# Zero fill of the first pair table from ScalarE's queue in group 0, and pair adds from group 9

## The reference, cut to what matters

```python
msg = relu(x[src] + edge_attr @ We + be)            # layer 0, graph
agg = segment_sum(msg, dst, num_segments=2500)
...
out = segment_sum((x @ W)[src] * norm, dst)         # layer 1: needs the count of (src, dst) in list 1
...
agg = segment_sum(h[src] * alpha, dst)              # layer 2, feed-forward: count of (src, dst) in list 2
```

## Time and profile before

| | |
|---|---|
| time before, median of 3 runs | 6491.18 us (6484.43 to 6493.86) |
| profiled execution, its own time | 6495.75 us |
| span of its profile | 6493.9 us |
| busy: PE, DVE, POOL, ACT | 5235.9, 3690.0, 3034.0, 1601.6 us |
| first `add` of the edges stage, last one | 83.94 us, 1697.36 us |

### The profile page before, as it was taken

The page is one execution under the profiler, slowest core; times in us unless marked ns, Lnnn a source line. Parts: engine busy times, 40 slices in busy tenths (PEclk is TensorE's granted clock), DMA queues, the critical chain, the costliest instruction groups (busy, mean ns, idle before and its releaser), DMA issues.

```text
span 6493.9 us, 83030 instructions
## 1 busy us (share of the span) xinstructions
PE 5235.9 (81%) x25932; PEld 3282.1 (51%) x25932; DVE 3690.0 (57%) x7654; ACT 1601.6 (25%) x2625; POOL 3034.0 (47%) x2048
## 2 busy tenths in 40 slices
PE   4677777777699898989569798776657998998899
PEld 3555555555455575558557566761113333222366
DVE  6777777787511202120235400979986997777732
ACT  1111111111222201220132121245541003555421
POOL 2577777788888878877777885000000000000000
PEclk8887887788799988999788699989988999999889
DMA  7765565644555596559799766944340001222100
GB/s 172 171 119 109 110 120 114 94 65 64 57 20 15 8 124 41 15 23 125 90 159 112 56 48 61 206 105 120 105 115 28 28 24 46 72 73 70 53 17 25
DMA packets 537605, 515.96 MB, mean 79 GB/s; under 512 B 262861, under 2 KB 494230, under 8 KB 531390
## 3 DMA queue, kind: packets, MB, share of 16 engines
q1 hardware_dynamic: 275694, 422.98, 29.8%
q0 software_dynamic: 261696, 90.13, 22.6%
HBM read 359.18 MB, written 153.71 MB: 79 GB/s over the span
## 4 chain that ended last, share of the span: by engine, by line
PE 46%; DVE 13%; issue 6%; SPq 5%; DMA 3%; ACT 1%; DVEq 0%; POOL 0%; ACTq 0%; POOLq 0%; PEldq 0%
PE PS L909 6%; PE PS L881 6%; PE PS L2033 6%; SPq L187 5%; PE PS L1901 5%; DVE WORK L1785 4%; PE PS L1270 4%; DVE MXS L1942 4%; PE PS L892 4%; PE PS L1562 3%; PE PS L1061 2%; PE PS L1050 2%; PE PS L245 2%; PE PS L1922 1%; PE PS L1252 1%
## 5 line engine op out<-in xcount | busy, mean ns | idle before, releaser
L642 POOL DMA_INDIRECT pairs<-PAIR_CNT,PAIR_IDX x1364 | 2159.8, 1583 | 559.1 <-issue 438.9
L469 DVE SCALAR_TENSOR_TENSOR XT<-PS,ROWS,XT 128x512 f32<-128x512 f32 (+1 forms) x1364 | 937.6, 743 | 148.1 <-PE PS L461 137.7
L999 DVE SCALAR_TENSOR_TENSOR X<-PS,G,X 125x256 f32<-125x256 f32 x440 | 193.0, 479 | 827.0 <-PE PS L909 786.2
L682 POOL DMA_INDIRECT sums<-WORK,ROWS x340 | 529.7, 1558 | 251.4 <-issue 189.0
L2088 DVE SCALAR_TENSOR_TENSOR WORK<-WORK 125x1000 f32<-125x1000 f32 x400 | 462.1, 1197 | 203.9 <-ACT WORK L2063 199.5
L1901 PE MATMUL PS<-ROWS 32*125 32x500 f32 x3200 | 455.8, 639 | 28.8 <-DVE MXS L1942 19.2
L1942 DVE TENSOR_REDUCE MXS<-PS 125x4 f32<-125x2000 f32 x200 | 438.8, 2235 | 41.6 <-PE PS L1922 37.6
L2063 ACT ACTIVATE WORK<-PS 125x1000 f32<-125x1000 f32 x400 | 380.0, 1002 | 329.3 <-PE PS L2023 329.3
L510 PE MATMUL PS<-WORK,IDENT 125*125 125x256 f32 x680 | 257.6, 467 | 237.9 <-DMA WORK<-x_table,WORK 237.7
L461 PEld LDWEIGHTS PS<-IDENT,ROWS 128*128 128x128 f32 (+1 forms) x2728 | 434.1, 226 | 30.0 <-issue 0.7
L461 PE MATMUL PS<-IDENT,ROWS 128*128 128x128 f32 (+1 forms) x2728 | 433.4, 312 | 0.0
(11 more groups left out here) (284 smaller groups left out, 7438.5 us busy)
## 6 DMA issues: line engine op xcount, KB each, us to landing
WORK<-pairs SPq DMA_DIRECT2D x400, 218.8 KB
pairs<-ROWS SPq DMA_DIRECT2D x75, 976.6 KB
WORK<-pairs SPq DMA_DIRECT2D x48, 1093.8 KB
WORK<-pairs SPq DMA_DIRECT2D x80, 546.9 KB
pairs<-PAIR_CNT,PAIR_IDX POOLq DMA_INDIRECT x1364
WORK<-pairs SPq DMA_DIRECT2D x40, 382.8 KB
XT<-pairs SPq DMA_DIRECT2D x12, 1093.8 KB
mask_t<-ROWS SPq DMA_DIRECT2D x40, 273.4 KB
```

The lines of the kernel that those rows point to most:

```text
L469: st.go(dve.scalar_tensor_tensor(KEY_JUNK[0:n, q, 0:SUPER * n], PS[0:n, bank, 0:SUPER * n], cols[0:n, q:q + 1], weights, ALU.is_equal, ALU ...
L642: pool.indirect_dma_start(table, bass.IndirectOffsetOnAxis(idx[:, n:n + 1], 0), cnt[:, n:n + 1], None, compute_op=ALU.add).then_inc(sem(do ...
L682: pool.indirect_dma_start(sums[c], bass.IndirectOffsetOnAxis(SROW[:, k % 8:k % 8 + 1], 0), SUMMED[:, k % 8, :], None, compute_op=ALU.add). ...
```

## The change

The 25 zero transfers of `pairs1` leave SP's loop. ACT issues them in group 0, after the copy of the sum of each step: 6, 6, 6 and 7 of them, with constant addresses. SP still issues the zero transfers of `pairs2` in the same iterations as before, and still the small one at the end of each table. `PG` is 9, not 13: three columns of list 1 are added in each of the groups 9 to 12 too, so `IN1` = 228, and 112 columns are left for `pairs_pool`.

```diff
-        PG, IN_GROUP = 13, 3
+        PG, IN_GROUP = 9, 3
...
+        def zero(eng, table, name, at):
+            rows = table[0:PAIRS, :].rearrange("(r p f) o -> r p (f o)", r=ZP, p=ZL)
+            rows = rows[at] if isinstance(at, int) else rows[ds(at, 1)].rearrange("r p f -> p (r f)")
+            eng.dma_start(rows, ZERO[0:ZL, 0:PAIRS // (ZP * ZL)]).then_inc(sem(name), 16)
...
             with sp.Fori(0, ZI) as i:
                 group(i * 2 + 1, 1)
                 group(i * 2 + 2, 0)
-                for n in range(ZP // ZI):
-                    zero(pairs1, "zeroed1", i * (ZP // ZI) + n)
...
                 for c in range(2):
-                    zero(pairs2[c], "zeroed2", i - ZI)
+                    zero(sp, pairs2[c], "zeroed2", i - ZI)
...
                     act.activation(SUMMED[0:P, s, :], PS[0:P, 4 + b, 0:AGG], ACT.Copy).then_inc(sem("sum_kept"), 1)
+                    if isinstance(g, int):
+                        for at in range(ZP * j // GR, ZP * (j + 1) // GR):
+                            zero(act, pairs1, "zeroed1", at)
```

More of the change, by code:

```diff
@@ L430, in edges_sp @@
                              ZERO[0:64, 0:2 * SUPER]).then_inc(sem("zeroed1" if table is pairs1 else "zeroed2"), 16)
-            def zero(table, name, at):
-                sp.dma_start(table[0:PAIRS, :].rearrange("(r p f) o -> r p (f o)", r=ZP, p=ZL)[ds(at, 1)]
-                             .rearrange("r p f -> p (r f)"), ZERO[0:ZL, 0:PAIRS // (ZP * ZL)]).then_inc(sem(name), 16)
             with sp.Fori(0, ZI) as i:
```

## The result

The changed kernel takes 6507.35 us (median of 17 runs, 6490.49 to 6523.03), the kernel before 6487.48 us (17 runs, 6466.78 to 6503.61): ratio 1.0033, interval 1.0021 to 1.0044. It is slower by a third of a per cent, some 20 us. That is inside the stated range (6478 to 6510) but not in the likeliest case; it fell to the 0.20 of "slower".

A forecast was written before the change was run, and what follows sets the result against it. POOL, saturated in the edges stage, was taken as the bound. Floor + 22.4 us, stall 91.6 to 69 = - 22.6, everything else 0: about 0, rounded to + 1, 6492 us on the median's scale; range 6478 to 6510.

The forecast's parts named there:

- the likeliest case: Whole kernel: a time within 0.2% of before, given 0.67.
- the 0.20 of "slower": Whole kernel: chance that it gets slower, from 0.09 + 0.10 for two rivals and 0.01 of the forecast's own spread.
- Both signs of being wrong: Fill burst and first 13 groups: steps not near 8 us, or stall not within some 10 us of 69.
- Who ends the stage, and that nobody waits for POOL later: Edges stage ends with POOL's last `add`; 22.4 us less POOL work after it is worth nothing.
- Twelve pair adds on the path: Groups 9 to 12, ahead of the last `add`: 12 x 1.87 = + 22.4 us.
- ScalarE's issues: Group 0, ACT's queue: 0.4 us for two zero transfers and 2.2 for 23, together 51 us.
- Steps in the burst: During the zero fill: POOL gets 10.5 steps done, at 8.2 us a step where its floor is 3.18.
- The step that failed: Groups 0 to 8: POOL's floor is 12.7 us a group, 114.5 us in all.
- The transfers have more time to drain: Groups 9 to 12: with pair adds between `add`s, `pairs2` zeroing costs 1.1 us a group, 4 us instead of 10.1.
- the stall did not go with the bytes: Rival on the fill: 16.3 us per 5 MB in any burst, stall 85.5, + 16 us, 6507; chance 0.10.
- POOL got no more room in a long burst: Rival on the fill: 5.5 us a step, 17 steps in the burst, - 19 us, 6472; chance 0.10.
- ScalarE was not held for the whole fill: Rival on ACT's queue: issues at drain pace hold ACT throughout, + 10 us, or + 26 at 226 GB/s; chance 0.18.

The follow-up runs named there:

- spread kernel: Also cited as (6): kernel before, PG = 13, each of SP's five `pairs1` zero transfers per iteration waiting for its own step; 6430.32 us, ratio 0.9929.
- 2: Changed kernel with PG back at 13, so only the zero fill from ScalarE remains, against the kernel before; 6496.32 us, ratio 1.0035.
- 5: Kernel before with PG = 85, no pair add in the edges stage, the wait for `zeroed1` moved to `pairs_pool`; 6968.36 us, one run.

## Why the prediction was right or wrong

The time lies in the range, but the mechanism isn't the one that was forecast, and that is in part luck. The forecast was a stall that shrinks from 91.6 to 69 us and so pays for the twelve pair adds. Counted in the same way, the stall after is 363.33 - 83.94 - 187.7 = 91.7 us: it didn't shrink at all. Both signs of being wrong that the prediction named have come, this one and the steps in the burst: 8 of them in the 98 us from 83.94 to 181.88, 12.2 us each and not near 8. The range reached up to 6510 for two rivals, and neither is what happened.

- **Who ends the stage, and that nobody waits for POOL later**: right. The slowdown is about the 17.9 us of the stage's end, and that POOL's last pair add came 21 us earlier bought nothing.
- **Twelve pair adds on the path**: right in kind. The prediction let groups 9 to 12 go from 61.0 to 73.2 + 4 = 77 us; they take 80.1.
- **ScalarE's issues**: 51 us predicted, 53.1 measured. Of the 25 MB, 20.06 went out in 90 to 175 us and the last 0.7 by about 182, near the forecast 180. The 6.27 us an issue, taken from the earlier trace rows for the pace of draining, were a misreading: it is the longest of four issues that took 13.68 us together, 3.4 each. The sum didn't use it.
- **Steps in the burst**: 10.5 predicted, with the ninth `add` (step 8) at 181.88 only 8 are done. That is 2.5 x 3.18 = 8 us. It is the hold: VectorE's row numbers of group 1 are missing for 23.5 us, VectorE waits for TensorE, and TensorE for the messages behind the issues (41.8 us).
- **The step that failed**: "Groups 0 to 8 cost 9 x 12.7 = 114.5 us". POOL runs at 12.7 only while VectorE is ahead of it, by at most the eight gathered buffers. In groups 2 to 4 it did; then groups 5 to 8 took 63.3 us, 12.5 more than that floor, at VectorE's pace, with the fill long over. 8 + 12.5 = 20.5 us is, to a fraction of a microsecond, the distance between the predicted start of group 9, 263 us, and the measured 283.3.
- The same step made the stall of before look like 91.6 us above the floor. Against VectorE's 16.0 a group it is 257 - 208 = 49 us, and the spread kernel took 45 of them. For groups 0 to 8, counted from 84 us against 9 x 16.0 = 144, the fill cost 52 us before, 55 after and 5 spread: one burst in place of five changed next to nothing. The rows had it: 677 us of VectorE's work in 47 groups is 14.4 us a group, above 12.7. They were read as "has room" because POOL needs 18.3 there.
- "The transfers have more time to drain" was a fair guess for the price of the `pairs2` transfers, 1.1 us a group, but no run shows that reason. The price came from two transfers in a row: four steps apart, groups 13 to 59 took 870.9 us against POOL's 860.1, 0.2 us a group.
- The rivals: the stall did not go with the bytes (6), and POOL got no more room in a long burst. ScalarE was not held for the whole fill, only for 59 of some 107 us.

Open: the fill alone (2) measured + 0.35%, 26 us between the medians, of which the stage's trace shows 11 to 15; the trace of before isn't of that experiment's series, in which the kernel before had a median of 6469.89 us, but of one with 6491.18. And the two halves alone, + 0.21% and + 0.35%, add up to more than the + 0.33% of both, though hardly outside their intervals. TensorE's granted clock moved along with the stalls: it was 0.71 in the burst, 0.80 in the first 13 groups before and 0.88 in the same groups of the spread kernel. What of the gain is the clock's, no run separates; where nothing is zeroed (5) it was 0.92, and VectorE was the limit.

## What to carry to other kernels

Before taking one engine's work per round as the floor, do the sum for each engine in the stretch at hand, above all where the change takes work from the one that bounds it now: here the next one was at 16.0 us a group, 26% above the 12.7 that was written down. Background transfers that share the DMA engines with short transfers on the path should go out one at a time, tied to the steps of the work; their bytes cost next to nothing here, but 2, 5 and 25 of them in a row did. On the queue of an engine that others wait for a burst costs more than that, since its issues hold the engine itself.

## What the runs showed of the hardware that was not expected

- Transfers in a row: groups 0 to 8 took 196.0 us with five bursts of five 1 MB transfers and 149.0 with the same 25 apart, 9.4 us a burst. Two of 1 MB in a row cost 40 us over 25 such pairs, apart almost nothing.
- An issue took 0.32 us on ScalarE's queue when the queue was free, 2.1 us on average in a burst of 1 MB transfers, 28 us on average for two of 2.5 MB whose transfers ran on about a third of the DMA engines.
- A burst that starves the engine with the least slack can't be made good afterwards: VectorE worked 48 of 109 us in it, and 57 of 63 us in the stretch from 220 us on, where it was the limit.
